# Windowed attention by head pairs: 64x64 score and value products instead of one head at a time

## The reference

```
q, k = rotary(rms_norm(x) @ w_q), rotary(rms_norm(x) @ w_k)     # 1024 x 64
scores = q @ [k of the own segment ; 32 extra keys].T / 8       # causal inside the segment
o      = softmax(scores) @ [v of the own segment ; 32 extra values]
x      = x + concat(o of 16 heads) @ w_out                      # then a gated feed-forward
```

## Time and profile before

| | us |
|---|---|
| median of 3 runs | 4444.05 (4439.82 to 4445.55) |
| the profiled execution, its own time | 4451.81 |
| its span, first to last instruction | 4449.9 |
| windowed attention, first score product to last output copy | 135.05 to 415.14 |
| its period, one head (score products at 250.66 and again at 267.82) | 17.16 |

### The profile page before, as it was taken

The page is one execution under the profiler, slowest core; times in us unless marked ns, Lnnn a source line. Parts: engine busy times, 40 slices in busy tenths (PEclk is TensorE's granted clock), DMA queues, the critical chain, the costliest instruction groups (busy, mean ns, idle before and its releaser), DMA issues. The chain is left out here.

```text
span 4449.9 us, 83947 instructions
## 1 busy us (share of the span) xinstructions
PE 3773.0 (85%) x34296; PEld 1305.2 (29%) x34358; DVE 3441.4 (77%) x3306; ACT 2843.8 (64%) x4073; POOL 258.4 (6%) x183
## 2 busy tenths in 40 slices
PE   6898479999999964899999999289837999999996
PEld 2554122222222222222222222145412222222221
DVE  4332289999999814999999994489838999999981
ACT  0332238888888851688888888145423888888884
POOL 3000100000000000000000000234410000000000
PEclk9555669999999985899999999699966999999998
DMA  2000411111111013111111100200040111111100
GB/s 90 1 0 0 81 18 26 26 18 22 26 26 26 3 29 76 24 21 19 26 26 26 26 14 4 56 11 5 3 86 14 26 26 23 16 26 26 26 4 21
DMA packets 54250, 113.98 MB, mean 26 GB/s; under 512 B 9424, under 2 KB 44368, under 8 KB 48912
## 3 DMA queue, kind: packets, MB, share of 16 engines
q1 hardware_dynamic: 53904, 109.09, 13.7%
HBM read 83.46 MB, written 25.50 MB: 24 GB/s over the span
## 5 line engine op out<-in xcount | busy, mean ns | idle before, releaser
L1541 DVE TENSOR_REDUCE chunk_max<-max_scores 128x2 f32<-128x988 f32 (+1 forms) x2496 | 2790.8, 1178 | 188.1 <-PE max_scores L1424 152.3
L1522 ACT ACTIVATE probs<-scores 128x512 f32<-128x512 f32 (+1 forms) x3231 | 2452.7, 808 | 531.1 <-PE scores L1450 508.6
L1477 PE MATMUL values_sum<-probs,values 128*9 128x256 f32 x19584 | 1375.6, 383 | 26.7 <-DVE values_sum_s L1552 18.5
L1450 PE MATMUL scores<-queries,key_ring 49*128 49x512 bf16 x4800 | 1230.3, 385 | 51.2 <-ACT probs L1522 18.3
L1424 PE MATMUL max_scores<-key_ring,queries 48*128 48x494 bf16 (+1 forms) x4992 | 984.3, 392 | 157.5 <-DVE chunk_max L1541 112.9
L1477 PEld LDWEIGHTS values_sum<-probs,values 128*9 128x9 f32 x19584 | 376.6, 89 | 788.3 <-issue 566.7
L1450 PEld LDWEIGHTS scores<-queries,key_ring 49*128 49x128 bf16 x4800 | 308.0, 94 | 642.5 <-ACT probs L1522 543.0
L1424 PEld LDWEIGHTS max_scores<-key_ring,queries 48*128 48x128 bf16 x4992 | 241.0, 94 | 852.6 <-DVE chunk_max L1541 545.0
L1061 ACT ACTIVATE probs<-scores 128x512 f32<-128x512 f32 x256 | 138.4, 592 | 106.1 <-PE scores L1013 106.1
L1087 DVE TENSOR_REDUCE chunk_max<-max_scores 128x1024 f32 (+1 forms) x128 | 154.9, 1214 | 24.5 <-PE max_scores L969 24.3
L1552 DVE COPY values_sum_s<-values_sum 128x256 f32<-128x256 f32 x48 | 20.0, 416 | 183.8 <-PE values_sum L1477 183.8
(11 more groups left out here) (179 smaller groups left out, 2055.7 us busy)
## 6 DMA issues: line engine op xcount, KB each, us to landing
key_ring<-k_parts SPq DMA_DIRECT2D x96, 300.2 KB
key_ring<-k_parts SPq DMA_DIRECT2D x96, 200.1 KB
k_parts<-k_part SPq DMA_DIRECT2D x108, 128.0 KB, 2.3
key_ring<-k_parts SPq DMA_DIRECT2D x96, 100.1 KB
o_whole<-values_sum_s SPq DMA_DIRECT2D x48, 128.0 KB, 7.1
queries<-q_parts SPq DMA_DIRECT2D x36, 128.0 KB
context<-in_ctx_t SPq DMA_DIRECT2D x1, 3202.0 KB, 17.5
q_parts<-q_part SPq DMA_DIRECT2D x12, 256.0 KB, 2.8
```

What stands on the lines that cost most here:

```text
L1450: return pe.matmul(sc[:, g % 3, :], keys(rows, h, P * t, P * (t + 1)), qb[rows, q], start=True, stop=True)
L1477: mm = pe.matmul(acc[32 * b:32 * b + WV, 0:QBLOCK], vb[rows, h, t, :], pr[rows, slot, QBLOCK * (b % 2):QBLOCK * (b % 2 + 1)], start=(t == ...
L1522: act.activation(pr[:, a % RING:a % RING + b - a, :], sc[:, a % 3:a % 3 + b - a, :], ACT.Exp)\
L1541: dve.tensor_reduce(mx[:, h % 2, c, :, j], mxb[:, w % 2, :, 0:width], AX.X, ALU.max)\
```

## The change

The attention works on pairs of heads. The two heads of a pair lie in partitions 0 to 63 and 64 to 127 of queries and keys (as before), and now of values too.

- Scores: for each tile, four products of 64 x 64 with 64 columns (two heads by two segments), each on its own quarter of the array: rows by head, columns by segment. Then two products 64 x 128 with the 32 extra keys, one per head. A tile of a head has 96 score columns, where it had 160.
- Turning: the probabilities of both heads lie side by side, so that one 128 x 128 transpose turns the own keys of both heads and one turns the extra ones (with zero columns between).
- Values: per tile four products of 64 x 64 with 64 columns, and per half four of 32 x 64 with 256 columns for the extra keys.
- DVE, ACT: the same operations on 96 columns per tile; the score buffer `sm` is gone, and the exponentials are taken in place in `probs`. The odd head of each pair is normalised by POOL, the even one by DVE, each in two operations (own, extra). ACT takes the exponentials of pair `s` in step `s`, not `s-1`. DVE copies a pair out after the masks and maxima of the next-but-two pair. POOL clears `pn` once at the start.
- Around it: values are projected by a phase of their own (`project_values`, 64 x 2 columns of tokens per segment, both halves of the heads side by side), the extra values too (`project_extra_values`), and the product with `w_o` is split in row halves (`project_windowed`). These three are `open_phase` phases, where `linear` was used. `w_o` comes by two loads.

The core of the diff:

```
-            def scores(h):
-                r = slice(DH * (h % 2), DH * (h % 2 + 1))
-                if h >= 1:
-                    pe.wait_ge(masked_ready, h)
+            def scores(p):
+                if p >= 1:
+                    pe.wait_ge(masked_ready, 2 * p)
                 for t in range(QT):
-                    q = qp[r, h // 2, P * t:P * (t + 1)]
-                    mm = pe.matmul(score[:, t, 0:WK], q, kp[r, h // 2, t, :], start=True, stop=True)
+                    for par in range(2):
+                        q = slice(P * t + SEG * par, P * t + SEG * (par + 1))
+                        for x in range(2):
+                            pe.matmul(score[x][SEG * par:SEG * (par + 1), t, 0:SEG], qp[head(x), p, q],
+                                      kp[head(x), p, q], start=True, stop=True)
+                    for x in range(2):
+                        mm = pe.matmul(score[x][:, t, SEG:WK], qp[head(x), p, P * t:P * (t + 1)], kx[head(x), p, :],
+                                       start=True, stop=True)
                 mm.then_inc(scores_ready, 1)
...
+            def turn(p, c):
...
+                pe.wait_ge(probs_even, p + 1)
+                pe.wait_ge(probs_odd, p + 1)
...
                 for t in range(4):
-                    pe.transpose(pt_tok[:, P * t:P * (t + 1)], pn[:, h % 2, 4 * c + t, NEX:WK], k.ident[:])
-                    mm = pe.transpose(pt_ext[0:NEX, P * t:P * (t + 1)], pn[:, h % 2, 4 * c + t, 0:NEX], k.ident[:])
+                    pe.transpose(pt_own[:, P * t:P * (t + 1)], pn[:, p % 2, 4 * c + t, 0, :], k.ident[:])
+                    mm = pe.transpose(pt_ext[:, P * t:P * (t + 1)], pn[:, p % 2, 4 * c + t, 1, :], k.ident[:])
                 mm.then_inc(turned, 1)
...
+            def values(p, c):
+                n = 2 * p + c
                 pe.wait_ge(turned_copied, 2 * (n + 1))
-                if h >= 2 and h % 2 == 0 and c == 0:
-                    pe.wait_ge(o_copied, h // 2)
+                if p >= 1 and c == 0:
+                    pe.wait_ge(o_copied, p)
                 for t in range(4):
-                    pe.matmul(o_bank[c][rows, P * t:P * (t + 1)], v_tok[:, 4 * c + t, DH * h:DH * (h + 1)],
-                              ptt[:, n % 2, P * t:P * (t + 1)], start=(t == 0), stop=False, skip_group_check=True)
-                pe.matmul(o_bank[c][rows, :], v_ext[:, DH * h:DH * (h + 1)], pte[:, n % 2, :],
-                          start=False, stop=True, skip_group_check=True).then_inc(o_ready, 1)
+                    for par in range(2):
+                        for x in range(2):
+                            at = P * t + SEG * par
+                            to = 4 * SEG * c + SEG * t
+                            pe.matmul(o_bank[x][SEG * par:SEG * (par + 1), to:to + SEG],
+                                      vs[head(x), 8 * c + 2 * t + par, DH * p:DH * (p + 1)],
+                                      own[head(x), n % 2, at:at + SEG], start=(c == 0 and t == 0), stop=False,
+                                      skip_group_check=True)
+                for par in range(2):
+                    for x in range(2):
+                        rows = extra(x)
+                        mm = pe.matmul(o_bank[x][SEG * par:SEG * (par + 1), 4 * SEG * c:4 * SEG * (c + 1)],
+                                       vx[rows, DH * p:DH * (p + 1)],
+                                       ext[rows, n % 2, :].rearrange("p (t s n) -> p t s n", s=2, n=SEG)[:, :, par, :],
+                                       start=False, stop=True, skip_group_check=True)
+                mm.then_inc(o_ready, 1)
+
+            for s in range(NPAIR + 2):
                 if s >= 2:
                     turn(s - 2, 0)
-                if s < H:
+                if s < NPAIR:
                     scores(s)
...
         @block.vector
...
+            dve.wait_ge(cleared, 1)
+            for s in range(NPAIR + 3):
+                if s < NPAIR:
                     mask_and_maximum(s)
+                if s >= 3:
+                    pair_out(s - 3)
+                if 1 <= s <= NPAIR:
+                    normalise_pair(s - 1)
+
+        @block.gpsimd
+        def _(pool):
+            pool.memset(pn[:], 0.0).then_inc(cleared, 1)
+            pool.wait_ge(cleared, 1)
+            for p in range(NPAIR):
+                pool.wait_ge(inv_ready, 2 * (p + 1))
+                if p >= 2:
+                    pool.wait_ge(turned, 2 * (p - 1))
+                normalise(pool, p, 1).then_inc(probs_odd, 1)
...
-            for s in range(1, H + 2):
+            for s in range(NPAIR + 2):
                 if s >= 2:
                     copies(s - 2, 0)
-                if s <= H:
-                    exps(s - 1)
+                if s < NPAIR:
+                    exps(s, 0)
                 if s >= 2:
                     copies(s - 2, 1)
+                if s < NPAIR:
+                    exps(s, 1)
...
+def project_windowed(k, w_o, o_pairs):
...
+            for h in range(H):
+                for par in range(2):
+                    rows = slice(SEG * par, SEG * (par + 1))
+                    mm = pe.matmul(bank[par][:], w_o[rows, h, :], o_pairs[rows, h // 2, HALF * (h % 2):HALF * (h % 2 + 1)],
+                                   start=(h == 0), stop=(h == H - 1))
+            mm.then_inc(projected, 1)
```

More of the change, by code:

```diff
@@ L61 @@
 NEX = 32
-WK = NEX + P
+WK = SEG + NEX
+NPAIR = H // 2
+NSEG = N // SEG
 DFF = 341
@@ L430, in windowed_projections @@
         linear(k, [(P, 16, [(w_qkv[:, H * DH + P * p:H * DH + P * (p + 1)], mem_tok[:, 0:16])])
[L431 to L437, removed]
+                   for p in range(NPAIR)],
@@ new lines, in windowed_projections, with project_values, _ @@
+               lambda e, n, b: e.tensor_copy(kx[:, n, 0:16], b))
+        project_extra_values(k, mem_tok, wv, vx)
+def project_values(k, xn, wv, vs, beside_vector):
+    nc = k.nc
+    with ExitStack() as ctx:
+        _, ps, sem = scope_tools(k, ctx)
+        bank = [ps("v_product", [P, HALF]) for _ in range(4)]
+        projected = sem("projected")
+        copied = sem("copied")
+        block = open_phase(k, ctx)
+        @block.tensor
+        def _(pe):
+            for g in range(NSEG):
+                if g >= 4:
+                    pe.wait_ge(copied, g - 3)
+                for half in range(2):
+                    mm = pe.matmul(bank[g % 4][DH * half:DH * (half + 1), :], xn[:, SEG * g:SEG * (g + 1)],
+                                   wv[:, HALF * half:HALF * (half + 1)], start=True, stop=True)
+                mm.then_inc(projected, 1)
+        @block.scalar
+        def _(act):
+            for g in range(NSEG):
+                act.wait_ge(projected, g + 1)
+                act.activation(vs[:, g, :], bank[g % 4][:], ACT.Copy).then_inc(copied, 1)
+        @block.vector
+        def _(dve):
+            beside_vector(dve)
@@ new lines, in project_extra_values, with _ @@
+def project_extra_values(k, mem_tok, wv, vx):
+    nc = k.nc
+    with ExitStack() as ctx:
+        _, ps, sem = scope_tools(k, ctx)
+        bank = ps("v_extra_product", [P, HALF])
+        projected = sem("projected")
+        block = open_phase(k, ctx)
+        @block.tensor
+        def _(pe):
+            for half in range(2):
+                mm = pe.matmul(bank[DH * half + NEX:DH * (half + 1), :], mem_tok[:], wv[:, HALF * half:HALF * (half + 1)],
+                               start=True, stop=True)
+            mm.then_inc(projected, 1)
+        @block.vector
+        def _(dve):
+            dve.wait_ge(projected, 1)
+            for half in range(2):
+                rows = slice(DH * half + NEX, DH * (half + 1))
+                dve.tensor_tensor(vx[rows, :], bank[rows, :], vx[rows, :], ALU.add)
@@ L563, in _ @@
             m3 = mask[:].unsqueeze(1).to_broadcast([P, QT, WK])
[L565 to L573, removed]
@@ new lines, in normalise_pair @@
+            def normalise_pair(p):
+                for x in range(2):
+                    dve.wait_ge(exp_ready, QT * (2 * p + x + 1))
+                    if x == 1 and p >= 2:
+                        dve.wait_ge(probs_odd, p - 1)
+                    dve.reciprocal(inv[:, p % 2, x, :], tot[:, p % 2, x, :]).then_inc(inv_ready, 1)
+                    dve.wait_ge(inv_ready, 2 * p + x + 1)
+                    if x == 0:
+                        if p >= 2:
+                            dve.wait_ge(turned, 2 * (p - 1))
+                        normalise(dve, p, x).then_inc(probs_even, 1)
@@ L610, in copies @@
+            def copies(p, c):
+                n = 2 * p + c
                 act.wait_ge(turned, n + 1)
```

166 lines of the change are left out of this document (92 added, 74 removed).

## The result

| | before | after |
|---|---|---|
| median | 4444.49 us (4 runs, 4439.82 to 4445.55) | 4347.57 us (4 runs, 4343.35 to 4350.91) |
| profiled execution, own time / span | 4451.81 / 4449.9 | 4350.91 / 4349.1 |
| first score product to last output copy | 135.05 to 415.14: 280.1 | 136.48 to 310.66: 174.2 |

The ratio of after to before is 0.9779, with a 95% interval of 0.9767 to 0.9792: 97 us faster, where 104 were predicted. The range and the predicted direction hold.

A forecast was written before the change was run, and what follows sets the result against it. TensorE was taken to bound the attention, busy 251.9 of 277 us at clock 0.50. Attention 105.6 us shorter (280.1 to 174.5) and +1.5 around it gave -104: median 4444 - 104 = 4340 us, range 4279 to 4402.

The forecast's parts named there:

- Four at once: Attention's 64x64 products: four quarters run simultaneously, 0.107 us a slot of 64 columns; all TensorE gain hangs on it.
- half-way rival: Attention quarters overlap only partly, through weight loads taking turns or limited record issue: 4375, 4402 or 4367 us; chance 0.18.
- the slower one (4513): Quarters in attention, value projection and w_o product do not overlap, columns stream one after another: 4513 us; chance 0.06.
- A change of shape costs 0.19, or 0.29 with an exposed load: TensorE in attention: price in us per change of array shape; sixteen in a pair's scores cost 3.8 us.
- The ring through `o_copied`: Attention: values wait for DVE's output copy behind masks and maxima, 4.9 us after scores; period 21.8 us against 34.3.
- Values and turn: TensorE in attention, per half: values 2.1 us where two heads cost 7.6, turn 1.9 where two heads cost 3.8.
- step 1: Attention pipeline's step with scores, masks and maxima, normalisation and POOL: 7.7 + 3.7 + 1.4 + 2.0 = 14.8 us.
- The stage: Whole attention, summed over steps 0 to 9: 174.5 us against 280.1, 105.6 less.
- step 2: Attention pipeline's step without `o_copied` wait, decided by exponentials: 1.9 + 7.7 + 7.2 + 2.1 + 1.9 = 20.8 us.
- Around it: Outside attention: value projection, extra values, w_o product, clearing blocks and loads, together +1.5 us.
- the likeliest case: The prediction's own case: median 4340 us, own range 4311 to 4365, attention clock at 0.50; chance 0.63.
- The 0.10 for its rising: Rival: granted clock rises in attention, halving all TensorE terms, 61 us less, 4279 us; chance 0.10.

The follow-up runs named there:

- quarter-by-quarter order: Kernel with all own score products ahead of the extra ones, own products reordered so 16 records in a row use one quarter: attention 189.7 us, median 4361.64 us.
- own products first: Kernel after, with each pair's own score products of all 8 tiles made before all extra ones: attention 146.6 us, median 4323.67 us.
- extra products 64 x 64: Kernel after, with extra-key scores as four 64x64 quarter products per tile instead of two with 128 weight columns: attention 133.7 us, median 4305.43 us.
- with 96 columns: Kernel after, with extra keys laid behind each segment's own keys, so one 96-column product replaces own and extra: attention 136.6 us, median 4304.58 us.
- all together: Kernel after, with 96-column products, DVE's output copy and ACT's copies moved first, and ten loads issued late: attention 102.0 us, median 4249.33 us.

## Why the prediction was right, point by point

- **Four at once** held, and decided it. Expected: own products of a tile in 0.40, change included. Measured: 0.42 (204.11 to 204.53). The quarter-by-quarter order shows what the other answer costs. The half-way rival and the slower one (4513) fall.
- **A change of shape costs 0.19, or 0.29 with an exposed load.** 14 changes less gave 2.4 us, where these prices give 7 x (0.19 + 0.12) = 2.2. The extra products took 0.57 a tile (204.53 to 205.10) against 0.56. A tile is 0.99 against 0.96, and the scores 7.95 against 7.7: the term of the period that was mis-sized. By the load time of the Trainium skill (TensorE: Matmul & The Clock Gate, LDWEIGHTS) the estimate for a tile was 0.76. The row on the 16-column products was the better guide.
- **The ring through `o_copied`**, 4.9 us of DVE and hand-overs: from 212.07, the end of the scores, to 217.06 it is 5.0, and moving the copy takes it out. TensorE's idle time before `values(s-2, 0)` is 4.99 with the predicted releaser, before `values(s-2, 1)` 1.18 with ACT as releaser, as said.
- **Values and turn**: 2.12 and 1.90 against 2.1 and 1.9. Period 22.2 against 21.8; over five periods, +2.
- **POOL** normalises the odd head in 1.04 + 0.62 = 1.66, not 1.9; it holds TensorE only before the first turn, for 6.8 us after the second scores, where the prediction's step 1 has 7.1.
- **The stage**: 174.2 against 174.5. That it is so close is luck, since the errors cancel: four periods at half clock were 0.4 longer each and the last two steps took 21.5 where 20.3 was predicted, but one period was 20.2 under the risen clock, and step 2 took 18.8 where 20.8 was predicted.
- **Around it**: the rotary projection took 0.9 less (56.7 against 57.6), not foreseen; the values' phase starts 3.99 behind the rotary products in both, and with its own clearing what follows it came 0.4 later (0.6 predicted); the pooled token's and extra keys' products took 0.7 less, not foreseen, because the clock stood at 1.0 until 129.1, where before it had fallen at 124.3; the extra values and their additions gave 0.6 (132.49 to 136.48 is 4.0; before, 130.42 to 135.05, 4.6), predicted 0.5; from the last output copy to the normalisation's first product it was 20.6 against 19.6, +1.1, predicted +1.3. Missed: the loads were costed at nothing, the second of w_o for having 300 us to land. Landing was hidden; the issues were not, since all engines wait for SyncE's last one: +3.3 us, of which w_o's two parts are 1.1.
- **The clock** stayed at 0.50 but for the two stretches from 248.6 to 252.0 and from 306.6 to 310.0, as the likeliest case had it. The argument for it misread a row: the 0.61 of the earlier trace rows is no rise in the extra-key products. The clock stood at 1.0 until 124.3, at 0.50 under those products, and at 1.0 again from 134.5, under the first scores of the kernel before, until 137.9; so it did not stay at 0.50 throughout the attention either. The 0.10 for its rising was not idle: with most or all changes of shape inside the scores gone, it stood at 1.0 for 24 to 51 us of the attention in four kernels, where it is 7 in the kernel after.

Of the 104 predicted, the profiled execution shows 100.9. The 3.3 of the loads is about that difference only because the other terms cancel: the rest up to the first score product came out 2.0 better than predicted, the part behind the product with `w_o` 2.6 worse. The medians differ by 96.9, because the execution profiled before lay 7.3 above its median and the one after 3.3 above. Behind the product with `w_o`, where the kernels are the same, the span after is 2.6 us longer (4017.8 from 331.30, against 4015.2 from 434.73). In the ten traces this part lasts 4010.6 to 4021.4, so 2.6 us is within the scatter of equal code. That stretches of high clock fall differently on the same work would explain the scatter; this is argued, not shown.

## What to carry to other kernels

Count shape changes of the array as instructions with a price: sixteen a pair at 0.17 us took back 2.7 of the 4.0 us that the overlap of four quarters gives in the scores, and keeping every product of the scores in one shape shortened the attention by another 40 us, part of it through the clock. After a change that makes the bounding engine faster, walk its semaphores once round: a copy that was hidden behind it may be ordered behind work that now depends on it, and a change of order alone then gives it back (17 us here, 27 with ACT's). A load that lands long before it is used still costs its issue, when a block waits for the issuing queue.

## What the hardware showed that was not expected

- Weight loads of 64 columns on the four quarters overlap as the products do: 16 records, loads included, in 0.43 us at half clock. In the kernel after, the eight own loads of the tile at 205.10 span 0.30 us.
- The granted clock stood at 1.0 for 24 to 51 us of the attention when the changes of shape inside the scores were gone or few (with own products first, with extra products 64 x 64, with 96 columns, and all together), and for 7 to 14 us in the kernel after and the edits that keep all of them. Yet with all edits together TensorE was busy 65.1 of 102.0 us, and before, when it stayed at 0.50 from 138 on, 91% of the time. It stayed at 0.50 in the quarter-by-quarter order, which differs from the first of these in the overlap alone. What makes it rise was not isolated.
- The clock gives and takes: the 96-column product saved records and no time, since the clock rose behind its scores and not within them.
- The issue of one DMA held SyncE's queue for 16 us, and 9 us when it was issued 15 us later, behind the same two large loads.
